# Gated cross-attention block: row loads and stores moved from GpSimd's queue to SyncE's, in one line with the context

## What is computed

```
x = x + tanh(g_xattn) * softmax(layernorm(x) @ ctx^T) @ ctx          # per batch, float32
x = x + tanh(g_ffn)   * (layernorm(x) @ W^T + bias)                  # W: 2048 x 2048
W = (unpacked 6-bit values of qweight - zero_point) * scale
```

## Time and profile before

| | us |
|---|---|
| median of 3 runs | 670.11 |
| lowest, highest | 667.25, 682.67 |
| profiled execution, its own time | 668.26 |
| its span, first to last instruction | 666.5 |

### The profile page before, as it was taken

The page is one execution under the profiler, slowest core; times in us unless marked ns, Lnnn a source line. Parts: engine busy times, 40 slices in busy tenths (PEclk is TensorE's granted clock), DMA queues, the critical chain, the costliest instruction groups (busy, mean ns, idle before and its releaser), DMA issues.

```text
span 666.5 us, 8134 instructions
## 1 busy us (share of the span) xinstructions
PE 607.7 (91%) x3240; PEld 392.1 (59%) x3240; DVE 392.8 (59%) x687; ACT 195.7 (29%) x391; POOL 58.2 (9%) x149
## 2 busy tenths in 40 slices
PE   0978999999699699969959998989999999999997
PEld 0877947947665694756559478445466444444443
DVE  2575636666375456728536675957676776563543
ACT  1544514514332350422235044223232131121000
POOL 3000000030013003001200300201200000000000
PEclk9997999999799899979989999989999999999999
DMA  8993058059829607912950692676843499394220
GB/s 250 273 285 101 1 162 282 12 180 255 308 68 305 181 0 217 266 71 87 302 165 1 226 299 106 210 220 185 285 157 83 143 252 253 90 247 106 83 68 35
DMA packets 39618, 113.64 MB, mean 171 GB/s; under 512 B 20974, under 2 KB 20974, under 8 KB 29422
## 3 DMA queue, kind: packets, MB, share of 16 engines
q1 hardware_dynamic: 18718, 83.54, 40.6%
q0 software_dynamic: 4224, 25.40, 12.7%
q10 hardware_dynamic: 16640, 4.20, 3.8%
HBM read 89.26 MB, written 19.66 MB: 163 GB/s over the span
## 4 chain that ended last, share of the span: by engine, by line
PE 77%; DMA 19%; DVE 2%; ACT 1%; SPq 1%; issue 1%; DVEq 0%
PE pv L812 24%; DMA raw<-in_ctx 17%; PE pv L863 17%; PE S L793 9%; PE S L863 8%; PE T L754 8%; PE S L795 5%; PE pv L754 4%; DMA raw<-in_L_ffn_qweight 2%; PE T L836 1%; PE S L876 1%; PE pv L876 1%; SPq L233 0%; ACT pT L435 0%; DVE stats L524 0%
## 5 line engine op out<-in xcount | busy, mean ns | idle before, releaser
L812 PE MATMUL pv<-raw,pT 128*100 128x512 f32 (+1 forms) x384 | 171.6, 597 | 2.5 <-ACT pT L436 2.5
L793 PE MATMUL S<-khi,qT 128*100 128x362 f32 x512 | 146.3, 368 | 0.0
L812 PEld LDWEIGHTS pv<-raw,pT 128*100 128x100 f32 (+1 forms) x384 | 62.3, 168 | 89.6 <-issue 85.8
L666 DVE TENSOR_TENSOR klo<-T,khi 128x361 fp32r<-128x361 f32 x128 | 67.7, 533 | 68.5 <-ACT khi L421 67.9
L754 PE MATMUL T<-ident,raw 128*128 128x128 f32 (+1 forms) x384 | 64.6, 284 | 31.7 <-DMA raw<-in_ctx 30.6
L421 ACT ACTIVATE khi<-T 128x361 fp32r<-128x361 f32 x128 | 60.0, 473 | 98.0 <-PE T L754 97.8
L795 PE MATMUL S<-klo,qT 128*100 128x362 f32 x256 | 87.3, 341 | 0.6 <-DVE klo L666 0.6
L666 DVE TENSOR_TENSOR klo<-pv,khi 128x361 fp32r<-128x361 f32 x128 | 67.6, 533 | 33.6 <-ACT khi L421 33.4
L754 PEld LDWEIGHTS T<-ident,raw 128*128 128x128 f32 (+1 forms) x384 | 52.3, 150 | 40.9 <-issue 37.3
L421 ACT ACTIVATE khi<-pv 128x361 fp32r<-128x361 f32 x128 | 60.0, 475 | 41.8 <-PE pv L754 41.3
L793 PEld LDWEIGHTS S<-khi,qT 128*100 128x100 f32 x512 | 71.6, 175 | 0.1
(11 more groups left out here) (88 smaller groups left out, 539.7 us busy)
## 6 DMA issues: line engine op xcount, KB each, us to landing
raw<-in_ctx SPq DMA_DIRECT2D x32, 1024.0 KB, 13.4
raw<-in_ctx SPq DMA_DIRECT2D x16, 840.0 KB, 14.9
raw<-in_L_ffn_qweight SPq DMA_DIRECT2D x16, 768.0 KB, 6.5
xres<-in_x POOLq DMA_DIRECT2D x8, 800.0 KB, 8.8
x_scratch<-xres POOLq DMA_DIRECT2D x8, 800.0 KB, 14.8
rows_scratch<-rows POOLq DMA_DIRECT2D x8, 800.0 KB, 12.6
raw<-x_scratch SPq DMA_DIRECT2D x24, 256.0 KB, 4.1
out_y<-raw SPq DMA_DIRECT2D x24, 256.0 KB, 2.5
```

The costliest lines, as they stand in the source:

```text
L666: dve.tensor_tensor(klo[:, slot, 0:GW], T[k][:, 0:GW], khi[:, slot, 0:GW].bitcast(F32), ALU.subtract).then_inc(s_free[k], 1)
L793: pe.matmul(S[0:R, g, 0:MW], qT[:, h, c, :], khi[:, slot, :], start=(c == 0 and h == 0), stop=False)
L812: last = pe.matmul(pv[n][0:R, :], pT[0:ROWS[t], t, :], raw[0:ROWS[t], b % 2, t, n * 512:(n + 1) * 512], start=(t == 0), stop=(t == NT - 1))
```

## The change

SyncE issues `next_x`, `x1_out`, `next_xres` and `rows_out`; GpSimd keeps `rs_out`, which now waits for the one before it each time. In SyncE's loop for batch b (which runs beside attend(b-2)) the order becomes: context tile 0, `next_xres(b-2)`, tiles 1 to 5, `rows_out(b-3)`, `next_x(b+1)`, `x1_out(b-2)`. `rows_out(i)` was issued beside attend(i+1) right after its scaling; it is now behind tile 5 there. At the start, x of batch 1 stands ahead of the second context, and the second context waits with it until the first queries are turned. In part two the row transfers are put between loads of weights and rows. On VectorE `unpack(1)` moves behind `rows_lo(1,1)`.

```
 @@ block.sync
+            def next_x(b):
+                k, u = bank("q", b - 1, 3)
+                sp.wait_ge(s_turned[k], u + 1)
+                sp.dma_start(xa[0:R, :], x[b]).then_inc(s_xa, 16)
+            def next_xres(i):
+                if i >= 1:
+                    sp.wait_ge(s_x1out, 16 * i)
+                    sp.wait_ge(s_mid, i)
+                sp.dma_start(xres[0:R, :], x[i]).then_inc(s_xres, 16)
+            def x1_out(i):
+                sp.wait_ge(s_x1, i * NCH + NCH)
+                sp.dma_start(x1_dram[i], xres[0:R, :]).then_inc(s_x1out, 16)
+            def rows_out(i):
+                sp.wait_ge(s_rows, i + 1)
+                sp.dma_start(rows_dram[i * R:(i + 1) * R, :], rows[0:R, :]).then_inc(s_rowsout, 16)
...
+            next_x(1)
             for t in range(NT):
                 load_ctx(1, t)
+            next_xres(0)
+            next_x(2)
             for b in range(2, B):
                 for t in range(NT):
...
                     load_ctx(b, t)
+                    if t == 0 and b >= 3:
+                        next_xres(b - 2)
+                if b >= 3:
+                    rows_out(b - 3)
+                if b < LAST:
+                    next_x(b + 1)
+                x1_out(b - 2)
...
+            def first_w(n):
+                sp.wait_ge(s_pvt, (LAST - 1) * (NT - 1) + n + 1)
+                load_w(n)
             load_rows(0)
             load_rows(1)
-            for n in range(2):
-                sp.wait_ge(s_pvt, (LAST - 1) * (NT - 1) + n + 1)
-                load_w(n)
+            first_w(0)
+            next_xres(LAST - 1)
+            first_w(1)
+            rows_out(LAST - 2)
             load_rows(2)
             load_w(2)
+            load_rows(3)
             load_w(3)
-            load_rows(3)
+            x1_out(LAST - 1)
+            next_xres(LAST)
             load_w(RT)
+            rows_out(LAST - 1)
             load_w(RT + 1)
+            load_w(RT + 2)
             load_rows(4)
-            load_w(RT + 2)
...
             for j in range(4):
                 load_x1(j)
+            x1_out(LAST)
+            rows_out(LAST)
             load_w(RT + 3)
 @@ block.gpsimd
             def rs_out(i):
                 pool.wait_ge(s_rs, i + 1)
-                if i == LAST:
-                    pool.wait_ge(s_rsout, 16 * LAST)
+                if i >= 1:
+                    pool.wait_ge(s_rsout, 16 * i)
...
             rstd(0, 0)
-            pool.dma_start(xres[0:R, :], x[0]).then_inc(s_xres, 16)
-            next_x(1)
             rstd(0, 1)
             for i in range(B):
-                if i + 2 < B:
-                    next_x(i + 2)
                 if i >= 1:
-                    x1_out(i - 1)
                     rstd(1, i - 1)
                 if i + 2 < B:
                     rstd(0, i + 2)
                 if i >= 1:
-                    next_xres(i)
-                    rows_out(i - 1)
                     rs_out(i - 1)
-            x1_out(LAST)
             rstd(1, LAST)
-            rows_out(LAST)
             rs_out(LAST)
 @@ block.vector
                     unpack(0)
                     rows_lo(1, 0)
+                    rows_lo(1, 1)
                     unpack(1)
-                    rows_lo(1, 1)
```

## The result

The changed kernel takes 637.98 us in the median of four runs (635.47 to 642.20), the kernel before 669.68 in the runs beside it. The ratio is 0.9545, with a 95% interval of 0.9471 to 0.9618: 4.5% faster. The profiled execution took 639.42 us with a span of 637.3; it is compared with the 668.26 and 666.5 of before. The forecast was 628.3, so the direction and the range of 621 to 648 held and the gain was less than forecast: 28.8 us between the two profiled executions where 40 were expected. (Some executions fell in a slower state: the profiled one of experiment 1, at a granted clock of 0.946 throughout, is left out of that experiment's time and used for its waits and landings alone.)

The account below looks back on a forecast made before the run. It took TensorE, held by five waits for late context tiles and their half clock, to bound the kernel. The terms summed as 668.26 - 36.5 + 3.5 - 2.8 - 4.2 = 628.3 us, range 621 to 648.

Parts of the forecast that it names:

- Row transfers behind the context: In the five middle steps, TensorE's wait for the last context tile goes, with its half clock: -36.5 us.
- I charge 0.7 us a step: Tiles 0 to 2 arrive 0.7 us before their need at A+22.1 (A: attend's start); that margin charged: +3.5 us.
- slow stretch: A+14 to A+20 (A: attend's start), about 6 us around the row sums' landing, counted at 158 GB/s.
- (a): Tile 2 comes 0.6 to 4 us late, xres spreading badly and row sums slowing more: 641 or 658 us; chance 0.22.
- The tiny stores: The 400-byte row-sum stores beside the attend, taken to slow the other packets for about 6 us.
- What waits behind: Transfers and waits queued behind others on SyncE and GpSimd are covered, next_xres by 1.7 us: cost nothing.
- The start: Row loads come after the first context, so TensorE's wait for its second half goes: -2.8 us.
- the swap: In attend(6)'s window, unpack(1) behind rows_lo(1,1) lets TensorE turn the first weight tile without a wait: -4.2 us.
- the rest of part two: The last window, 218.85 us, keeps its instructions: 0, with ends -1 and +4.
- (b): Context was slow of itself, so only the start and the swap pay: 661 us; chance 0.04.
- (d): A wait in part two replaces the gains there, +4 to +10: 632 to 638 us; chance 0.10.
- (c): SyncE's line blocks: in next_xres the centring or x1's landing ends late, holding five tiles; at A+20, 694 us; chance 0.02.

Follow-up runs that it names:

- experiment 1: Changed kernel with the 400-byte row-sum stores of batches 0 to 4 issued some 28 us later: 628.37 us, ratio 0.9365.
- experiment 5: Changed kernel with late row-sum stores and the xres load cut at row 96: 623.31 us, ratio 0.9288.
- experiment 3: Changed kernel with each xres load cut into rows 0 to 95 and 96 to 99: 633.61 us, ratio 0.944.
- experiment 7: Changed kernel with each row sum stored in a row of 512 bytes instead of 4, same queue and moment: 629.58 us, ratio 0.9376.
- experiment 8: Kernel before with late row-sum stores and unpack(1) behind rows_lo(1,1), row transfers left on GpSimd's queue: 643.57 us, ratio 0.9585.
- experiment 6: Kernel before with only unpack(1) moved behind rows_lo(1,1): 665.24 us, ratio 0.9919.
- experiment 2: Changed kernel with the xres load behind context tile 2 instead of tile 0: 648.19 us, ratio 0.967.

## Why the prediction was right, and where it was off

*What bounded the kernel* was right: TensorE with five waits for context and their half clock. The window without a wait, 49.08 us, was the floor; in the profiled execution of experiment 5 it is reached in every step (49.05 to 49.09).

*Row transfers behind the context* had the right sign. No wait for tile 5 is left. In step one that is owed to the wait before: tile 5 landed 15.0 us after its issue, at about A+37, which would have been late for A+33.8; in the others it took 9.5 to 11.0 us. The term that failed is its charge, "tiles 0 to 2 are there at A+21.4 ... I charge 0.7 us a step": tile 2 came at A+27.5 in the first and A+24.0 in the second of the steps, and the charge measured 14.7 us over five windows instead of 3.5. Put into the sum, it is 628.3 - 3.5 + 14.7 = 639.5, where the profiled execution took 639.42; the small differences of the other terms cancel.

Why it was short: it counted the bytes of a tile at a mean rate over all engines. It took the slow stretch as a lower rate (158 GB/s from A+14 to A+20), where the measured rates are 246 GB/s to A+20 and 168 after it. It had the row sums land within some 6 us of their issue; they took 14.8, 12.5, 11.7, 11.8 and 10.5. So the slow stretch lasted until tile 2 was needed, and the prediction's own sign for (a), a wait at the first piece, is what the trace shows. Rival (a) named place and cause. Its price in sum, 16 us and a time of 641, was near the 14.7 us and 639.42 measured, but not its shape: 3.2 us of wait in each step, where it was 5.48 in the first and 0.9 to 2.1 in the others. It had too little of a chance. The spread over ten engines, which it also brought in, is not shown by experiment 3. The charge of 0.7 us a step came from no row: it was the margin itself, written down once more. A margin that small, on a need that the whole step hangs on, should have moved the forecast itself, not only the range.

*The tiny stores* as the cause of the slow stretch were taken from one coincidence of a landing and a rate. Experiments 1, 7 and 8 show it. What the prediction did not draw from it is that moving them alone takes some 22 us off the kernel before (experiments 6 and 8), as much as the move of the row transfers did with the tiny stores left where they were (36.5 - 14.7 = 21.8).

*What waits behind* held: the centring let `xres` go at 194.06, A+5.3, and tile 1 followed at its release at 195.86. *The start* came 3.2 us earlier (2.8 forecast), *the swap* was 4.1 (4.2 forecast) and shown alone, *the rest of part two* 0.1 (0 forecast). Rivals (b) and (d) are out by the windows, (c) by the issue times just named.

Still open: why the first of the five steps waits 5.48 us and the others 0.9 to 2.1. Tile 1 was late there too, 18.7 us after its issue where step two has 11.1. The same step is the longest of experiment 2, but not of experiment 3.

## What to carry to other kernels

When competing transfers are put into one line, look at each tile's own deadline, and at the earliest one too: curing the last tile can make an early one late. Keep stores of a few bytes a row (4 here) to device memory away from the stretch in which a deadline hangs on other transfers, or give each piece 512 bytes. A load that is needed soon, but not first, may do better on a second queue that shares than anywhere in the line.

## What the runs showed of the hardware that was not expected

- A store of 100 pieces of 4 bytes, 400 bytes in all, costs other transfers microseconds. Moved away it gave some 10 us (637.98 to 628.37), with pieces of 512 bytes in the same place some 8 (629.58), and in the kernel before, with the swap in both, 22 (665.24 to 643.57).
- With such stores in flight, 246 and then 168 GB/s moved from A+14 to A+20 and on to A+24, and tile 2 took 13.5 us to land, though more bytes had moved than stood ahead of its end; in experiment 5, without them, it was 270 and 381 GB/s and 9.6 us.
- With the same 0.82 MB load cut into rows 0 to 95 and 96 to 99, one execution had 5.2 us less of waits over five steps, 4.1 of it in one step.
- Waits of 2.06 and 2.57 us left the clock at full, but not every one of that length did: in experiment 8 the step with a wait of 2.02 us has a mean clock of 0.97, with 2 us at 0.50 of full speed right after, and in experiment 3 the one with a wait of 2.94 us is 53.67 us long at 0.97. A wait of 5.48 us brought the window to 0.94.
